# Joining retrieval, state-space and context-attention stages of a decoder kernel into one loop over steps

## What is computed

```python
def _L2_ffn_ref(hidden_states, Wq, keys, down_embed, up_embed, Wg, Wu, Wd):   # retrieval
    q = hidden_states @ Wq.T                          # to 2 halves, 4 heads, 64
    sim = jnp.einsum('pbthn,hkpn->pbthk', q, keys)    # 128 keys a half
    sx, ix = jax.lax.top_k(sim[0], 8); sy, iy = jax.lax.top_k(sim[1], 8)
    # the 8 best of the 64 sums sx + sy give, per head, scores and indices in 0..4095
    w = jnp.einsum('btd,bthkd->bthk', hidden_states, down_embed[indices])
    w = jax.nn.silu(w) * jax.nn.softmax(scores, axis=-1)
    experts_states = jnp.einsum('bthk,bthkd->btd', w, up_embed[indices])
    mlp = jax.nn.silu(hidden_states @ Wg.T) * (hidden_states @ Wu.T) @ Wd.T
    return mlp + experts_states

def _L3_attn_ref(x, ...):                             # state-space
    u, v = split(x @ in_proj_w + in_proj_b); v = jax.nn.silu(v)
    # v_local: convolution of 3 taps along the tokens; h = a*h + ssm_b*v_local; y = ssm_c*h + ssm_d*v_local
    out = (u * jax.nn.silu(y_seq)) @ out_proj_w + out_proj_b
    return layernorm(out + x) * ln_w + ln_b

def _L3_xattn_ref(x, context, Wq, Wk, Wv, Wo, bo):    # context attention, 8 heads of 64, 120 keys
    attn = jax.nn.softmax(jnp.einsum('bhid,bhjd->bhij', q, k) * scale, axis=-1)
    return jnp.einsum('bhij,bhjd->bhid', attn, v).reshape(B, Sq, h * d) @ Wo + bo
```

## Time and profile before

| | |
|---|---|
| timed runs, us | 3117.63, 3112.78, 3108.11; median 3112.78 |
| span of the profiled execution, us | 3106.5 |
| what the timed runs lie above that span | 1.6 to 11.1 |
| TensorE clock granted, mean of the span | 0.885 |
| busy share: TensorE, VectorE, ScalarE, GpSimd | 75%, 52%, 31%, 25% |
| gathers of L2f: busy, mean | 523.7 us, 1023 ns, 512 of them |

### The profile page before, as it was taken

How to read it: one execution, slowest core, us unless ns; L and a number is a source line. 1 busy time by engine, 2 the same in 40 slices (tenths; PEclk the granted TensorE clock), 3 DMA queues, 4 the chain that set the end, 5 groups by cost and what they waited for, 6 DMA issues and landing times. The chain is left out here.

```text
span 3106.5 us, 37880 instructions
## 1 busy us (share of the span) xinstructions
PE 2320.2 (75%) x13729; PEld 1493.0 (48%) x13729; DVE 1607.0 (52%) x4352; ACT 963.3 (31%) x1784; POOL 787.0 (25%) x755
## 2 busy tenths in 40 slices
PE   6877699888777655485677674877777877689786
PEld 3544378735443432462244333666666664237332
DVE  3754300067545657246374666655665544533486
ACT  0132222210241322132114463443334334424343
POOL 1000200041001006451000004777777771000000
PEclk9999699989998877796899897988889889899898
DMA  7200244337006142553500106222222221000000
GB/s 183 63 21 2 99 149 172 143 85 177 11 18 176 38 159 108 182 179 128 94 5 23 69 1 152 66 55 56 53 55 58 62 53 37 0 29 1 1 0 27
DMA packets 126828, 232.20 MB, mean 75 GB/s; under 512 B 38777, under 2 KB 76537, under 8 KB 122560
## 3 DMA queue, kind: packets, MB, share of 16 engines
q1 hardware_dynamic: 73552, 125.12, 14.2%
q0 software_dynamic: 51952, 100.65, 11.0%
q10 hardware_dynamic: 1152, 4.19, 0.3%
HBM read 245.59 MB, written 66.72 MB: 101 GB/s over the span
## 5 line engine op out<-in xcount | busy, mean ns | idle before, releaser
L3192 POOL DMA_INDIRECT L2f_G<-in_L2f_table,L2f_idx x512 | 523.7, 1023 | 288.7 <-issue 155.2
L3249 PE MATMUL psum<-L2f_G,L2f_diag 128*128 128x256 f32 x1024 | 304.4, 463 | 168.8 <-ACT L2f_diag L3319 168.8
L3249 PEld LDWEIGHTS psum<-L2f_G,L2f_diag 128*128 128x128 f32 x1024 | 235.9, 236 | 234.8 <-ACT L2f_diag L3319 192.0
L3427 DVE CUSTOM_DVE_ANT_0 L2f_junk<-L2f_G,L2f_X 128x256 bf16<-128x256 f32 x512 | 182.8, 421 | 254.0 <-DMA L2f_G<-in_L2f_table,L2f_idx 253.9
L3319 ACT ACTIVATE L2f_diag<-const,L2f_actd 128x128 f32<-128x128 f32 x528 | 161.1, 388 | 24.2 <-DVE L2f_actd L3441 24.2
L1191 PE MATMUL psum<-constb 128*128 128x256 bf16 x512 | 81.0, 282 | 96.8 <-ACT L1a_PT L1358 24.6
L2669 POOL DMA_INDIRECT picks_x<-L1f_rows,L1f_put x64 | 71.0, 1109 | 242.1 <-ACT L1f_rows L2759 223.2
L3226 PE MATMUL psum<-xT,L2f_mw 128*128 128x256 f32 x512 | 123.2, 385 | 0.0
L3312 ACT ACTIVATE L2f_actd<-L2f_dots 128x9 f32<-128x9 f32 (+1 forms) x64 | 13.5, 211 | 316.3 <-DVE L2f_dots L3427 316.3
L1358 ACT ACTIVATE L1a_PT<-psum 128x1536 f32<-128x1536 f32 x32 | 46.4, 1450 | 205.5 <-PE psum L1326 205.5
L1191 PEld LDWEIGHTS psum<-constb 128*128 128x128 bf16 x512 | 41.0, 99 | 142.2 <-ACT L1a_PT L1358 32.9
(11 more groups left out here) (689 smaller groups left out, 4882.8 us busy)
## 6 DMA issues: line engine op xcount, KB each, us to landing
L1f_we<-in_L1f_w SPq DMA_DIRECT2D x32, 384.0 KB, 8.2
picks_x<-zeros SPq DMA_DIRECT2D x16, 544.0 KB, 9.1
L1f_xe<-picks_x SPq DMA_DIRECT2D x32, 272.0 KB, 2.9
picks_y<-zeros SPq DMA_DIRECT2D x16, 512.0 KB, 6.4
L2f_G<-in_L2f_table,L2f_idx POOLq DMA_INDIRECT x512, 2.8
slots_x<-zeros POOLq DMA_DIRECT2D x8, 512.0 KB, 7.6
L1f_wb<-in_L2x_w SPq DMA_DIRECT2D x1, 4096.0 KB, 12.2
L1f_g<-picks_y ACTq DMA_DIRECT2D x8, 512.0 KB, 11.9
```

What stands on the lines that cost most here:

```text
L3192: nc.gpsimd.indirect_dma_start(out=G[:, h, k, :], out_offset=None, in_=ins["L2f_table"], in_offset=bass.IndirectOffsetOnAxis(ap=IDX[:, t, ...
L3249: mm = nc.tensor.matmul(ps[:, MIX_BANK + t % 2, 0:D], diag[:, i % 2, k, :], row[:, D:2 * D], start=(h == 0 and k == 0), stop=(h == HEADS - ...
L3427: e = V.tensor_tensor_reduce(out=junk[:, k, :], in0=row[:, 0:D], in1=X[:, t % 3, :], scale=1.0, scalar=0.0, op0=ALU.mult, op1=ALU.add, acc ...
```

## The change

`peer_tail_stage` replaces the retrieval stage, its norm, the state-space stage and the context attention. One loop of 81 steps (`END`) runs on each engine. Steps 0 to 63 hold the retrieval steps as before. A sequence is two tiles, eight steps. From step 9 on, sequence m goes through the norm of the retrieval, the state-space part and its two norms in eight pieces d = 0 to 7, one a step (`ssm_at`); from step 17 on a sequence goes through context attention and its norm in sixteen pieces z, two a step (`cross_at`: z = 2d and 2d + 1). Both work in chunks of 256 columns:

| d | `ssm` | `cross`, first and second piece |
|---|---|---|
| 0 | mean, subtraction, Square | 0 keys and values; 1 queries |
| 1 | variance, Ln, Exp, Square, Newton | 2 scores, maxima; 3 maxima turned |
| 2 | input projection, Silu | 4 turned scores, Exp; 5 values and sums, Ln, Exp, product |
| 3 | convolution, scan, Silu | 7 scores, maxima (second four heads) |
| 4 | product U*S, output projection, residual | 8 maxima turned; 9 turned scores, Exp |
| 5 | variance, Ln, Exp, Square, Newton, scaling | 10 values and sums, Ln, Exp, product |
| 6 | mean, subtraction, Square | 12 output projection, residual, Square; 13 variance, Ln, Exp, Square, Newton |
| 7 | as 1 | none |

On TensorE a step is: first attention piece, turn_back, similar or queries, state-space piece, picks(i), wait for gated(i), down(i), up(i+1), second attention piece. `up` now has one PSUM bank, which `similar` and the token copy of `queries` also use. On ScalarE: keep, weigh, diagonal, first attention piece, route copies, state-space piece, second attention piece, the route's Exp, gate(i+1). On VectorE: gated(i), dot(i), first attention piece, weighted(i) (ahead of piece 10), add_mix, add_dense, state-space piece, a third of the route, second attention piece. The gather buffer has 28 rows in a ring instead of 32 by head. Some VectorE operations of the route that ran once a head now run once for all heads. SP loads the attention's weights at the start and those of `L3f` in the last 17 steps. No table set is asked for by name in the new function. The diff, cut to its core:

```diff
-STAGES = ["L0a", "L0x", "L0f", "L1a", "L1x", "L1f", "L2a", "L2x", "L2f", "L3a", "L3x", "L3f"]
+STAGES = ["L0a", "L0x", "L0f", "L1a", "L1x", "L1f", "L2a", "L2x", "L2f", "L3f"]
...
+    LATER = 2 * PER + 1
+    END = LATER + PER * (B - 1) + PER
+    ROWS = 28
+    HELD = 8
...
+        def ssm_at(i):
+            m, d = divmod(i - PER - 1, PER)
+            return (m, d) if 0 <= m < B else (0, None)
+
+        def cross_at(i, part):
+            m, e = divmod(i - LATER, PER)
+            return (m, 2 * e + part) if 0 <= m < B else (0, None)
+
+        UNIT = {2: 0, 3: 0, 4: 0, 5: 0, 7: 1, 8: 1, 9: 1, 10: 1}
...
+                sp.wait_ge(s["pk_used"].sem, s["pk_used"].at(STEPS))
+                sp.wait_ge(s["pk_part"].sem, s["pk_part"].at(STEPS))
+                c.load_last(sp, 0)
+                sp.wait_ge(s["q_proj"].sem, s["q_proj"].at(B))
+                c.load_last(sp, 1)
...
+                for i in range(STEPS):
+                    t, h = divmod(i, HEADS)
+                    if h == 0:
+                        pool.wait_ge(s["pk_routed"].sem, s["pk_routed"].at(t + 1))
+                    for k in range(TOPK):
+                        n = i * TOPK + k
+                        if n >= ROWS and (k == 0 or (n - ROWS) % TOPK == 0):
+                            pool.wait_ge(s["pk_used"].sem, s["pk_used"].at((n - ROWS) // TOPK + 1))
+                        nc.gpsimd.indirect_dma_start(
+                            out=G[:, n % ROWS, :], out_offset=None, in_=ins["L2f_table"],
+                            in_offset=bass.IndirectOffsetOnAxis(ap=IDX[:, t % HELD, h * TOPK + k:h * TOPK + k + 1], axis=0),
+                            bounds_check=EXPERTS - 2 if t else None, oob_is_err=False)\
+                            .then_inc(s[got[h]].sem, 16)
...
+                def cross(i, part):
+                    m, z = cross_at(i, part)
+                    u = UNIT.get(z)
+                    if z == 0:
...
+                    if z == 1:
+                        pe.wait_ge(s["k_evac"].sem, s["k_evac"].at(m + 1))
+                        pe.wait_ge(s["v_evac"].sem, s["v_evac"].at(m + 1))
+                        pe.wait_ge(s["x_ready"].sem, s["x_ready"].at(2 * m + 2))
+                        for g in range(GH):
+                            for j in range(DH):
+                                mm = mm_(ps[:, CROSS + g // 2, half_of(g % 2)], wx["wq"][:, j * 512 + g * P:j * 512 + g * P + P],
+                                         c.xT[:, j, chunk(m)], start=(j == 0), stop=(j == DH - 1))
+                        mm.then_inc(s["q_proj"].sem, 1)
...
+                    if z in (5, 10):
+                        pe.wait_ge(s["probs"].sem, s["probs"].at(2 * m + u + 1))
+                        for j, k in pairs:
+                            h = 2 * (2 * u + j) + k
+                            mm_(ps[hc(k), CROSS, half_of(j)], Vc[0:CTX, h * HC:(h + 1) * HC], PT[0:CTX, k, half_of(j)],
+                                start=True, stop=True, skip_group_check=True)
+                        for j, k in pairs:
+                            mm = mm_(ps[hc(k), CROSS2, half_of(j)], ones[0:CTX, :], PT[0:CTX, k, half_of(j)],
+                                     start=True, stop=True, skip_group_check=True)
...
+                for i in range(END):
                     t, h = divmod(i, HEADS)
-                    if i + 1 < STEPS:
-                        up(i + 1)
-                    if h == 0 and t + 2 < NT:
-                        queries(t + 2)
-                    picks(i)
-                    if i:
-                        down(i - 1)
-                    if h == 0 and t + 2 < NT:
-                        similar(t + 2)
-                    if h == 0 and t:
+                    cross(i, 0)
+                    if h == 0 and 0 < t <= NT:
                         turn_back(t - 1)
-                down(STEPS - 1)
-                turn_back(NT - 1)
+                    if i < STEPS:
+                        if h == 1 and t + 2 < NT:
+                            pe.wait_ge(s["pk_hid"].sem, s["pk_hid"].at(i + 1))
+                            pe.wait_ge(s["pk_yadd"].sem, s["pk_yadd"].at(t))
+                            similar(t + 2)
+                        if h == 2 and t + 3 < NT:
+                            pe.wait_ge(s["pk_hid"].sem, s["pk_hid"].at(i + 1))
+                            queries(t + 3)
+                    ssm(i)
+                    if i < STEPS:
+                        picks(i)
+                    if i < STEPS:
+                        pe.wait_ge(s["pk_hid"].sem, s["pk_hid"].at(i + 1))
+                        down(i)
+                        if h == 1 and t + 2 < NT:
+                            pe.wait_ge(s["pk_sime"].sem, s["pk_sime"].at(t + 3))
+                        if h == 2 and t + 3 < NT:
+                            pe.wait_ge(s["pk_qe"].sem, s["pk_qe"].at(t + 4))
+                        if i + 1 < STEPS:
+                            up(i + 1)
+                    cross(i, 1)
...
+                def inverse_root(bank, root, square, done):
+                    link(nc.scalar.activation(root, ps[:, bank, 0:CW], ACT.Ln, bias=c.eps))
+                    link(nc.scalar.activation(root, root, ACT.Exp, scale=-0.5))
+                    nc.scalar.activation(square, root, ACT.Square).then_inc(s[done].sem, 1)
+
+                def ssm(i):
+                    m, d = ssm_at(i)
+                    if d == 0:
+                        act.wait_ge(s["d_ready"].sem, s["d_ready"].at(2 * m + 1))
...
+                    if z in (4, 9):
+                        act.wait_ge(s["masked"].sem, s["masked"].at(2 * m + u + 1))
+                        nc.scalar.activation(PT[0:CTX, :, :], ps[0:CTX, CROSS:CROSS + 2, :], ACT.Exp, scale=SCALE).then_inc(s["probs"].sem, 1)
+                    if z in (5, 10):
+                        act.wait_ge(s["mixed"].sem, s["mixed"].at(2 * m + u + 1))
+                        link(nc.scalar.activation(inv[:, :], ps[:, CROSS2, :], ACT.Ln))
+                        nc.scalar.activation(inv[:, :], inv[:, :], ACT.Exp, scale=-1.0).then_inc(s["inverted"].sem, 1)
...
+                for i in range(END):
                     t, h = divmod(i, HEADS)
-                    weigh(i)
-                    diagonal(i)
+                    if h == 0 and 0 < t <= NT:
+                        keep(t - 1)
+                    if i < STEPS:
+                        weigh(i)
+                        diagonal(i)
+                    cross(i, 0)
+                    if i < STEPS:
+                        if h == 1 and t + 2 < NT:
+                            evac_similar(t + 2)
+                        if h == 2 and t + 3 < NT:
+                            evac_queries(t + 3)
+                    ssm(i)
+                    cross(i, 1)
+                    if i < STEPS and h == 3 and t + 2 < NT:
+                        exps(t + 2)
                     if i + 1 < STEPS:
                         gate(i + 1)
...
+                def newton(bank, root, square, t, y, out):
+                    link(VE.scalar_tensor_tensor(t, ps[:, bank, 0:CW], EPS, square, ALU.add, ALU.mult))
+                    link(VE.scalar_tensor_tensor(t, t, -3.0, root, ALU.add, ALU.mult))
+                    return VE.scalar_tensor_tensor(out, y, -0.5, t.unsqueeze(1).broadcast_to([P, DH, CW]), ALU.mult, ALU.mult)
...
+                    if d == 5:
+                        dve.wait_ge(s["root_ready"].sem, s["root_ready"].at(3 * m + 2))
+                        link(newton(SSM2, aroot, asquare, anewton, L[:, :, :], L[:, :, :]))
+                        for k in range(DH):
+                            e = VE.scalar_tensor_tensor(L[:, k, :], L[:, k, :], wa["lw"][:, k:k + 1], c.xT[:, k, chunk(m)],
+                                                        ALU.mult, ALU.add)
+                        e.then_inc(s["normed"].sem, 1)
...
+                    if z in (5, 10):
+                        dve.wait_ge(s["inverted"].sem, s["inverted"].at(2 * m + u + 1))
+                        VE.tensor_tensor(AT[:, 2 * u:2 * u + 2, :], ps[:, CROSS, :].rearrange("p (g q) -> p g q", g=2),
+                                         inv[:, :].rearrange("p (g q) -> p g q", g=2), ALU.mult).then_inc(s["at_ready"].sem, 1)
...
+                for i in range(END):
                     t, h = divmod(i, HEADS)
-                    dot(i)
-                    if h == 1 and t:
+                    if i < STEPS:
+                        gated(i)
+                    ssm_gate(i)
+                    if i < STEPS:
+                        dot(i)
+                    late = cross_at(i, 0)[1] == 10
+                    if not late:
+                        cross(i, 0)
+                    if i < STEPS:
+                        weighted(i)
+                    if late:
+                        cross(i, 0)
+                    if h == 0 and 0 < t <= NT:
                         add_mix(t - 1)
                         if t % 2 == 0:
                             add_dense(t // 2 - 1)
```

(46 more changed lines are left out.)

884 lines of the change are left out of this document (367 added, 517 removed).

## The result

The changed kernel takes 3375.18 us, the median of four runs (3371.66 to 3386.57); beside it the kernel before took 3114.17. The ratio is **1.0847**, 95% interval 1.0823 to 1.0872: 8.5% slower. The forecast was 3387. The profiled execution took 3386.57 us, its span 3384.7, with a granted clock of 0.849; it was the slowest of the four.

What follows compares the result with a forecast made beforehand. GpSimd's gathers (10.6 us a step) bound the kernel before; joined, a 12.9 us program-order ring would. Terms 37 + 142 + 130 + 895 + 120 = 1324 against 1050, +274 us, gave 3387 us, range 3240 to 3470.

Steps and rivals of the forecast that it cites:

- steps 17 to 63: Joined steps holding retrieval, state-space and attention: six eights of 152.8 us less one step of kind 7 (21.5), 895 us.
- The ring of 12.9 us: Program-order chain across engines, dots through picks, down, up, gate to next dots: 12.9 us a step empty, against gathers' 10.6.
- kind 5: Step d=5 of eight: four table loads, Newton, scaling and best_keys delay the next dots, adding 6.6 us (8.3 fast).
- Eight steps: One full period of joined steps: 8 x 12.94 + 34.3 for new pieces + 15 for the clock = 152.8 us.
- the clock term: TensorE's picks slow after idle: +1.7 us for gaps of 2 to 3.5 us, +2.7 above; 15 us per eight steps.
- Two loads for Ln and Exp: ScalarE, no set named: one 1.28 us load between Ln and Exp, about 21 loads per eight steps; chance 0.68.
- The rival "one load": The set loaded ahead of Ln also serves Exp: 7.7 us less per eight steps, 45 in all, 3342 us; chance 0.13.
- The fast-clock rival: New pieces fill TensorE's gaps, keeping it at 2.4 GHz: eight steps 143 us, 3284 in all; chance 0.07.
- The sign "most blocks at 5.4 us or more": Sign that the forecast is right: most of TensorE's picks blocks in the joined stage last 5.4 us or more.
- The last 17 steps: Steps 64 to 80, without retrieval: attention and state-space chains with short TensorE bursts at low clock, 120 us (82 to 150).
- the chain of 42 us: In steps 64 to 80, one sequence of attention is a chain of some 42 us by the same prices.
- The deciding mean step of 14.0 us: Mean over the 64 retrieval steps, (1050 - 37 - 120) / 64 = 14.0 us; below that the change is faster.

Runs made afterwards that it cites:

- e5: Changed kernel with TensorE's up(i+1) ahead of picks(i) in two steps of four, ScalarE's gate(i+1) right after the diagonals: 3284.37 us, ratio 1.0556.
- f3: Changed kernel with ScalarE's gate(i+1) ahead of its second attention piece and VectorE's second piece behind the next dots: 3301.88 us, ratio 1.0597.
- e7: Changed kernel with VectorE's third of the route ahead of the state-space piece in kinds 1, 5 and 7: 3357.67 us, ratio 1.0787.
- e6: Changed kernel with four edits: one named Ln/Exp set, gate and dots ahead of second attention piece, early up, route ahead of state-space piece: 3122.78 us, ratio 1.0023.
- e1: Changed kernel with a set holding Ln and Exp named ahead of each Ln: 3377.86 us, ratio 1.051, on a chip where the kernel before took 3215.26.
- f2: Same kernel as e1 (changed kernel, Ln/Exp set named ahead of each Ln), run on another chip: 3346.02 us, ratio 1.0741.
- f4: e6 plus VectorE's weights of the picks ahead of its first attention piece in every kind: 3096.39 us, ratio 0.9939.

## Why the prediction was right

Joined stage, forecast and measured (first dot at 1925.6; picks of steps 9, 17 and 63 at 2071.75, 2202.17 and 3064.89; step 63's down ends at 3072.1; the 6.7 from first dot to first picks and the 7.2 behind the last stand with steps 17 to 63):

| part | forecast | measured |
|---|---|---|
| start to first dot | 37 | 34.7 |
| steps 0 to 8 | 142 | 139.5 |
| steps 9 to 16 | 130 | 130.4 |
| steps 17 to 63 | 895 | 876.6 |
| steps 64 to 80 | 120 (82 to 150) | 136.7 |
| sum | 1324 | 1317.9 |

- **The ring of 12.9 us** held. Without attention and state-space work (steps 0 to 8) a step takes 15.6 (forecast 15.5), of which 2.3 is the clock in the picks (forecast 2.6). e5, f3 and e7 each cut the ring at the place named and gained. e7's kind 5 gave its price (3.9), f3 10.3 in eight steps for 12, and e5 more than its price, since more had left the ring than I counted. GpSimd idles with the picks as releaser, VectorE before `gated` with the Silu of h.
- **Eight steps**: 150.2 against 152.8. The blocks of picks lasted, up to the start of down, 3.56, 4.95, 5.24, 5.40, 4.95, 5.25, 5.39 and 5.86 us in kinds 0 to 7 (steps 25 to 32), 12.1 us over eight of 3.56. Kinds 3 and 7 hold two products more, for the ninth row, 0.43 us each (such a block took 3.99 in kinds 3 and 7 of e6), so that the clock term measured 11.2; I took 15, as 1.7 and 2.7 a block where 1.4 to 1.9 came. The rest, 139.0, was forecast as 137.8. By kind, less the surplus of the block, kinds 0 to 5 measure 18.0, 14.9, 19.5, 15.3, 17.2 and 19.8 against 18.5, 14.6, 19.0, 15.5, 17.2 and 19.5; kinds 6 and 7 measure 18.6 and 14.8 against 17.7 and 13.3; the forecast kept 2.2 of long rows outside the kinds. Six kinds were right to 0.5 us, the other two to 0.9 and 1.5, so not only the mean was.
- **Tables.** Two loads for Ln and Exp, forecast against the rule of one: 21 loads in eight steps and 165 in all (about 21 and 150). What the Trainium skill, "ScalarE: Activation LUTs", Table sets, says (Ln then Exp is one load) holds here only where the set is named: 14 loads in eight steps in e1 and f2, 21 in the changed kernel. The drain of about 1380 ns a switch that the same page of the Trainium skill gives under What ACT_TABLE_LOAD costs doesn't show: Exp starts 1.30 us after its load starts (2397.84, 2399.14) as in rows 5. The rival "one load" had the wrong price: I counted 7.7 us in eight steps, and f2 gave 3.4, since the named load, behind the wait, costs what the load between Ln and Exp had cost, and the load it replaced ahead of the wait had cost nothing.
- **The clock.** The granted clock was 0.85 on average in steps 16 to 63: after idle of 1.39 us a block took 3.56 us, after 2.91 us 4.95, after 9.17 us 5.39 (and after 2.27 us 5.24: the idle time just ahead does not order them alone). The fast-clock rival fell, though not by the argument that I gave against it: idle of 9 us or more stands ahead of one block in eight (9.17), not three. The sign "most blocks at 5.4 us or more" came true by the rows' own durations, which run to the end of the last product, as 5.41 in rows 3 does: 31 of the 46 blocks of steps 17 to 62, and 20 of the 35 that have 16 products.
- **The last 17 steps** were mis-sized, 136.7 for 120. The term was the chain of 42 us for a sequence of attention: the last one runs alone from 3147.58 to 3208.8, 61 us, with the mean clock at 0.67. Its two projections of 16 products took 5.76 and 5.41 us instead of 3.6, values and sums 3.7 twice instead of 2.05, the turned scores 3.0 and 3.8 instead of 1.9: 10 us of the 19. Keys and values ahead of them took another 10.6, and the forecast names no price for them. I had said "low clock" and priced the high one. The nine steps with both kinds of work took 75.5.
- **Steps 17 to 63** were forecast 18 too long: the eight steps by 2.6, nearly six times, is 15 (the clock term 3.8 too much, the rest 1.2 too little); step 63, which has no up behind it, is in the remainder. The sum takes off 21.5 for a step of kind 7, which by the forecast's own prices is 12.9 + 0.4 + 1.1 + 2.6 = 17.0 (measured 17.1). With that the stretch would have been 900 and the forecast 3391.
- **Luck** is in the nearness of the sum: 18 too much in steps 17 to 63 and 17 too little behind them cancelled. The ring and the kinds do not rest on it.
- **The side to which the sum fell.** The deciding mean step of 14.0 us was right too, first dot to the end of step 63's down over 64: the changed kernel has 17.9, e6 has 13.98 ((2817.9 - 1923.3) / 64) at a ratio of 1.0023, and f4 13.5 ((2792.0 - 1925.6) / 64) at 0.9939.

The forecast median is 12 us above the measured one: 6 in the joined stage, the rest in adding to the span of one execution: the span profiled before lay 6.3 under the median to which I added, the execution profiled after took 11.4 more than its median.

## What to carry to other kernels

When work is merged into a loop to fill idle engines, first write down, across all engines, the ring that leads from one iteration's result to the next in program order, and put the length of that ring beside the bound: 12.9 us against 10.6 decided this before any new work was counted. Work inserted between two members of the ring costs its full time unless another branch into the next member is longer. Moved one position later it may cost nothing (kind 4 of f3, 4.5 us less) or come back in the next step (kind 3 of f3, 1.4 us more). Before pricing such a move, follow the ring again: in e5 the picks themselves left it. The order is tuned one member at a time: issue what starts the next ring (up, gate, product) ahead of what merely has to be done.
